# Reordering the opening of a cross-attention and expert kernel: the second key sums, the norms' product, the first tile's values

## The reference

```
q, k, v = ln(x) @ Wq.T + bq,  ctx @ Wk.T + bk,  ctx @ Wv.T + bv      (16 heads of 8)
scores = where(mask, float_min, q @ k.T / sqrt(8))                    (1024 x 6404)
x = x + (softmax(scores) @ v merged) @ Wo.T + bo
x = x + experts(ln(x))      (top 2 of 8, hidden width 512, gelu)
```

## Time and profile before

| | us |
|---|---|
| median of 3 runs | 332.46 (331.86 to 334.14) |
| the profiled execution | 330.95 |
| its span, first to last instruction | 329.3 |
| busy in the span: PE / DVE / ACT / POOL | 267.3 / 176.7 / 230.0 / 80.5 |

### The profile page before, as it was taken

One profiled execution on the slowest core, in us unless ns is written; L12 is line 12 of the kernel. 1 busy time (PEld: TensorE's weight loads), 2 busy tenths in 40 slices (PEclk: granted clock), 3 DMA queues, 4 the chain that ended last, 5 costly groups with the idle time before them and its releaser, 6 DMA issues.

```text
span 329.3 us, 6448 instructions
## 1 busy us (share of the span) xinstructions
PE 267.3 (81%) x1941; PEld 134.8 (41%) x1944; DVE 176.7 (54%) x431; ACT 230.0 (70%) x366; POOL 80.5 (24%) x137
## 2 busy tenths in 40 slices
PE   2689978989999989898989898966777577799940
PEld 2455534122121212121222222254666577798940
DVE  4799864354535363535454535476963125677612
ACT  4458856999999999999999999716951212555520
POOL 8891013000000000100010004030387105344430
PEclk9999999999999999999999999999979597999995
DMA  7999580101010101010100101895011521100115
GB/s 214 360 402 404 195 178 6 41 2 40 0 40 12 28 12 28 12 28 14 26 21 19 26 14 28 304 317 89 17 49 51 145 57 35 32 29 30 34 36 187
DMA packets 29011, 29.31 MB, mean 89 GB/s; under 512 B 15341, under 2 KB 22913, under 8 KB 28864
## 3 DMA queue, kind: packets, MB, share of 16 engines
q1 hardware_dynamic: 27536, 26.21, 26.2%
q0 software_dynamic: 1456, 2.86, 2.9%
HBM read 21.62 MB, written 7.45 MB: 88 GB/s over the span
## 4 chain that ended last, share of the span: by engine, by line
PE 45%; ACT 19%; issue 16%; DVE 11%; DMA 3%; another core or an unknown queue 2%; DVEq 2%; ACTq 1%; POOL 0%; POOLq 0%; SPq 0%
PE bank L1385 12%; ACT w2T L1073 10%; PE bank L1367 7%; PE bank L1494 6%; PE bank L1502 3%; PE bank L1235 3%; ACT arenaB L1073 3%; PE bank L1512 2%; PE bank L1196 2%; DVE arenaB L949 1%; PE bank L1261 1%; ACT w1T L1099 1%; ACT w2T L1099 1%; DMA x_sb<-in_x_dram 1%
## 5 line engine op out<-in xcount | busy, mean ns | idle before, releaser
L756 DVE TENSOR_TENSOR arenaA<-bank,arenaA 128x512 f32<-128x512 f32 x80 | 55.2, 691 | 80.0 <-PE bank L1385 80.0
L1073 ACT ACTIVATE arenaB<-bank 128x1024 f32<-128x1024 f32 x80 | 77.5, 1021 | 2.8 <-PE bank L1367 0.7
L1073 ACT ACTIVATE w2T<-bank 128x1024 f32<-128x1024 f32 x80 | 76.6, 1029 | 3.4 <-PE bank L1367 2.9
L1367 PE MATMUL bank<-qS,keys 64*128 64x512 bf16 x328 | 62.7, 386 | 10.7 <-ACT w2T L1073 7.6
L1106 ACT ACTIVATE mask_u<-bank,arenaB 128x128 f32<-128x128 f32 x92 | 26.3, 369 | 46.5 <-PE bank L1494 41.7
L1367 PEld LDWEIGHTS bank<-qS,keys 64*128 64x128 bf16 x328 | 15.5, 92 | 98.0 <-ACT w2T L1073 51.4
L1385 PE MATMUL bank<-arenaB,vcur 128*32 128x512 f32 x320 | 42.6, 604 | 2.8 <-DVE vcur L749 2.6
L1385 PE MATMUL bank<-w2T,vcur 128*32 128x512 f32 x320 | 42.6, 605 | 0.0
L411 POOL CAST keep<-flags 128x1 f32 x12 | 2.3, 189 | 161.1 <-DVE arenaC L649 139.6
L1494 PE MATMUL bank<-arenaB 128*128 128x128 f32 x184 | 28.1, 302 | 10.9 <-DVE arenaB L941 9.9
L1494 PEld LDWEIGHTS bank<-arenaB 128*128 128x128 f32 x184 | 24.7, 209 | 13.2 <-DVE arenaB L941 11.9
(11 more groups left out here) (318 smaller groups left out, 349.0 us busy)
## 6 DMA issues: line engine op xcount, KB each, us to landing
mask_u<-in_L_ffn_w_dram SPq DMA_DIRECT2D x2, 2048.0 KB, 10.5
mask_u<-in_mask_BxSxS_bk_dram SPq DMA_DIRECT2D x6, 560.5 KB, 12.6
ctx_sb<-in_ctx_dram SPq DMA_DIRECT2D x3, 768.0 KB, 13.4
qS<-qparts_dram SPq DMA_DIRECT2D x4, 448.0 KB
mask_u<-in_mask_BxSxS_bk_dram SPq DMA_DIRECT2D x6, 240.0 KB, 10.8
keys_in<-kparts_dram SPq DMA_DIRECT2D x40, 32.0 KB
mask_u<-in_mask_BxSxS_bk_dram SPq DMA_DIRECT2D x1, 1121.0 KB, 7.5
qparts_dram<-arenaA SPq DMA_DIRECT2D x2, 512.0 KB, 8.1
```

The costliest lines, as they stand in the source:

```text
L756: nc.vector.tensor_tensor(a, bank[:, 4 + k % 2, :], a, ALU.add).then_inc(s["ac"], 1)
L1073: nc.scalar.activation(probs[u % 8], bank[:, 2 * (u % 2):2 * (u % 2) + 2, :].rearrange("p a b -> p (a b)"), ACT.Exp, scale=SCALE).then_inc ...
L1367: last = mm(bank[:, 2 * (u % 2) + a, :], keys[rows, g, :], qS[rows, g, cols], start=not hides, stop=True, tile_position=(64 * a, 0))
```

## The change

The change reorders the stretch between the last chunks and the loop.

- The second key sums stand ahead of the last chunk's product (step 13 instead of 14) and lose the three fill-in matmuls around them.
- ScalarE no longer clears a part of `accU` at step 11: groups 1 to 3 are cleared in one instruction behind the last chunk.
- The norms' product stands ahead of the first tile's keys.
- The first tile's values are made behind L1284 in bank 3 (columns 128 to 255) instead of bank 6 behind the loads; VectorE's `value_parts` takes the place to read from as an argument, and its copy `vsrow` out of the same bank waits for `kv` too.
- The two loads stand ahead of the second half of `first_keys`.
- `hide(1)` stands behind `products(0)` and waits for the values (`vn`) and `cs_sb`.

```diff
--- before.py
+++ after.py
@@ -642,16 +642,16 @@
                 dve.wait_ge(read, i * 16 * KEY_DMAS + 16 * KEY_DMAS)
                 nc.vector.tensor_copy(keys[:, :, :].bitcast(F32), keys_in[:, :, :].bitcast(F32)).then_inc(copied, 1)
 
-            def value_parts(i):
+            def value_parts(i, products):
                 dve.wait_ge(s["kp"], 2 * i + 2)
                 dve.wait_ge(s["kv"], i + 1)
                 nc.vector.tensor_copy(vnext[:, :, HD:HD + 1], keep[:, :].rearrange("p (h a) -> p h a", h=1).broadcast_to([P, H, 1]))
-                nc.vector.scalar_tensor_tensor(vnext[:, :, 0:HD], b6[:, 2 * P:3 * P].rearrange("p (h d) -> p h d", d=HD), keep[:, :],
+                nc.vector.scalar_tensor_tensor(vnext[:, :, 0:HD], products.rearrange("p (h d) -> p h d", d=HD), keep[:, :],
                                                bvk[:, :].rearrange("p (h d) -> p h d", d=HD), ALU.mult, ALU.add).then_inc(s["vn"], 1)
 
             def parts(i):
                 key_parts(i, s["kv"], i + 1, s["kch"])
-                value_parts(i)
+                value_parts(i, b6[:, 2 * P:3 * P])
 
 
             dve.wait_ge(s["bd_ps"], 2)
@@ -678,12 +678,13 @@
             dve.wait_ge(s["rowkey"], len(COMBOS) + 4)
             nc.vector.tensor_tensor(shift_col[:, :], bank[:, 2, 64:65], shift_rows[:, :], ALU.mult).then_inc(s["bias"], 1)
             dve.wait_ge(s["cs_ps"], 1)
+            dve.wait_ge(s["kv"], 1)
             nc.vector.tensor_copy(vsrow[:, :], bank[0:1, 3, 0:P]).then_inc(s["cs_sb"], 1)
             dve.wait_ge(s["mt"], 2)
             nc.vector.tensor_copy(maskT[:, 0, :], maskT_ps).then_inc(s["mc"], 1)
             dve.wait_ge(s["cs_ps"], 2)
             nc.vector.tensor_copy(vsumB[:, :], bank[:, 3, 0:P]).then_inc(s["cs_sb"], 1)
-            value_parts(0)
+            value_parts(0, bank[:, 3, P:2 * P])
             dve.wait_ge(s["gen_ready"], 1)
             partial = dve.value_load(plan[0:1, 66:67], min_val=0, max_val=T)
             n = dve.value_load(plan[0:1, 64:65], min_val=1, max_val=T)
@@ -1025,9 +1026,6 @@
             for c in range(CHUNKS + 1):
                 if c == 1:
                     zero_sums(0, 1)
-                if c == 11:
-                    act.wait_ge(s["q_sb"], 4)
-                    zero_sums(1, 2)
                 if c == 2:
                     act.wait_ge(s["qk_ps"], 2)
                     nc.scalar.activation(ext[:, 0:2 * XE + QT * E], bank[:, 7, 0:2 * XE + QT * E], ACT.Copy).then_inc(s["qk_sb"], 1)
@@ -1049,9 +1047,10 @@
                     if c >= 3:
                         act.wait_ge(s["kn_ps"], c - 2)
                     nc.scalar.activation(squares[:, (c - 1) % 2, 0:w], bank[:, 6 + (c - 1) % 2, 0:w], ACT.Square, bias=qk_col[:, 1:2]).then_inc(s["sqr"], 1)
+            act.wait_ge(s["q_sb"], 4)
             act.wait_ge(s["qw"], 16 * len(Q_RUNS))
             act.wait_ge(s["qn_ps"], 1)
-            zero_sums(2, 4).then_inc(s["ac"], 1)
+            zero_sums(1, 4).then_inc(s["ac"], 1)
             act.wait_ge(s["plan_ready"], 1)
             first = act.value_load(plan[0:1, 0:1], min_val=0, max_val=T - 1)
             act.wait_ge(s["bd"], 7)
@@ -1217,13 +1216,12 @@
                     pe.wait_ge(s["qk_sb"], 2)
                 if c == 10:
                     key_sums(0)
-                if c == CHUNKS + 1:
+                if c == CHUNKS:
                     pe.wait_ge(s["kb_sb"], 1)
                     pe.wait_ge(s["bd"], 1)
                     pe.wait_ge(s["pick"], 1)
-                    keep_busy(bank[:, 2, :], 2)
                     key_sums(1)
-                    keep_busy(bank[:, 7, :], 1)
+                if c == CHUNKS + 1:
                     plan_counts()
                 if c < CHUNKS:
                     context_turn(c)
@@ -1275,13 +1273,15 @@
 
             pe.wait_ge(s["plan_ready"], 1)
             tile0 = pe.value_load(plan[0:1, 0:1], min_val=0, max_val=T - 1)
+            pe.wait_ge(s["bd"], 6)
+            mm(bank[0:1, 2, 0:H], norms[:, 2:3], ident[0:H, 0:H], start=True, stop=True).then_inc(s["bd_ps"], 1)
             pe.wait_ge(s["cc_sb"], CHUNKS)
             mm(b6[:, P:2 * P], wk_turned[:, :], ctx_sb[:, bass.ds(tile0, 1), :].rearrange("p a k -> p (a k)"), start=True, stop=True).then_inc(s["k_first"], 1)
-            pe.wait_ge(s["bd"], 6)
-            mm(bank[0:1, 2, 0:H], norms[:, 2:3], ident[0:H, 0:H], start=True, stop=True).then_inc(s["bd_ps"], 1)
             pe.wait_ge(s["cs_sb"], 1)
             pe.wait_ge(s["pl_sb"], 15)
             mm(bank[0:1, 3, 0:P], csT[:, :], wT[:, 2, :], start=True, stop=True).then_inc(s["cs_ps"], 1)
+            pe.wait_ge(s["cb"], 1)
+            mm(bank[:, 3, P:2 * P], cT[:, :], wT[:, 2, :], start=True, stop=True).then_inc(s["kv"], 1)
 
             def first_keys(g0, g1):
                 for gg in range(g0, g1):
@@ -1301,12 +1301,10 @@
             pe.wait_ge(s["s2"], 1)
             mm(bank[:, 3, 0:P], ones[0:1, 0:P], vsrow[0:1, :], start=True, stop=False)
             mm(bank[:, 3, 0:P], s2row[0:1, :], brow[0:1, 2, :], start=False, stop=True).then_inc(s["cs_ps"], 1)
-            first_keys(4, G)
             pe.wait_ge(s["gen_ready"], 1)
             partial = pe.value_load(plan[0:1, 66:67], min_val=0, max_val=T)
             general = pe.value_load(plan[0:1, 65:66], min_val=0, max_val=1)
-            pe.wait_ge(s["cb"], 1)
-            project_values().then_inc(s["kv"], 1)
+            first_keys(4, G)
             with pe.If(general):
                 n_max = pe.value_load(plan[0:1, 64:65], min_val=1, max_val=T)
                 pe.wait_ge(s["mc"], 1)
@@ -1388,12 +1386,13 @@
 
             pe.wait_ge(s["mc"], 1)
             hide(0, 0)
-            pe.wait_ge(s["cs_sb"], 3)
-            hide(1, 0)
             pe.wait_ge(s["qr"], 64)
             pe.wait_ge(s["qzero"], 2)
             pe.wait_ge(s["kc"], 1)
             products(0, True)
+            pe.wait_ge(s["cs_sb"], 3)
+            pe.wait_ge(s["vn"], 1)
+            hide(1, 0)
             products(1, True)
             pe.wait_ge(s["kc"], 2)
             pe.wait_ge(s["vn"], 1)
```

## The result

| | before | changed |
|---|---|---|
| median of runs, us | 332.16 (331.14 to 334.14, 4 runs) | 328.35 (328.05 to 328.86, 4 runs) |
| profiled execution, us (span) | 330.95 (329.3) | 328.86 (327.2) |
| busy share PE, DVE, ACT, POOL | see the section on the profile before | 82, 54, 70, 25% |

The ratio of the mean times is 0.988, with a 95% interval of 0.9831 to 0.9928. By the medians the change gains 3.8 us (2.4 to 5.6 by the interval); I had forecast 2.45, 330.0, and a range whose low end was 328.7. The direction was right, the size was not. Chips differ more than the kernels do: the unchanged kernel takes 320 us on two of them. Disturbed executions, some per cent slower, are left out of the ratios, and one chip has so many in every kernel (near 330, beside some near 320 to 324) that it gives none.

The account below looks back on a forecast made before the run. Bound taken: a chain of exponentials on ScalarE, so each microsecond won before the first one, at 54.20, comes off the end. 1.77 - 0.10 + 0.33 + 0.45 = 2.45 us, 332.46 to 330.0; range 328.7 to 332.0.

Parts of the forecast that it names:

- Plan 1.77 earlier: End of the chunk stage: memset moved and key sums earlier make the plan of tiles ready 1.77 us earlier, at 44.5.
- A matmul's wait holds the sequencer: Plan to first mask matmul: the values' product waits for POOL's copy and delays TensorE's sequencer steps behind it, cost 0.1 us.
- Rival 1: Plan to loop: a matmul's wait does not hold the sequencer, so loads and branch come sooner; gain 3.0, 329.5 us; chance 0.15.
- the forecast of 1.67 for L1295: Plan to first mask matmul: L1295 starts at 47.2 against 48.89, 1.67 us earlier, where the rest would have allowed 1.8.
- Loads ahead of the 24 instructions, +0.33: Before the branch: loads ahead of the first keys' second half save 0.84, less 0.1 and 0.4 for handing over: 0.33 us.
- the 2.0 forecast: Before the hides: semaphore step that lets ScalarE copy the keys at 50.25 to 50.4 against 52.3, first hide 2.0 us earlier.
- Second hide, +0.45: Loop's start: two hide matmuls instead of four stand before the first products, 0.45 us more gained.
- Rival 4: Opening, 42 to 45 us: without three fill-ins TensorE's clock falls to 1.2 GHz; slower by 4.5, 337 us; chance 0.04.
- Rivals 2 and 3: Loads lie bare 1.3 us before the keys' second half, 331.3, chance 0.12; a later wait takes the gain, 332.2, 0.12.
- the hand-over: TensorE's sequencer before the branch: 24 instructions handed over at 0.013 to 0.02 us each; 26 ns each takes 0.3 off.

Follow-up runs that it names:

- loads_late: Changed kernel with its two loads put back behind the second half of the first keys: 330.58 us, ratio 0.9966.
- after_fill: Changed kernel with six more fill-in matmuls between the second key sums and the tile's number: 328.55 us, ratio 0.9833; on a quieter chip 318.10, 0.9921.
- end_only: Kernel before with only the end of the chunk stage changed (memset, key sums, fill-ins): 321.43 us, ratio 1.0027; again on another chip 321.25, 0.9997.

## Why the prediction was wrong in size

- **Plan 1.77 earlier: right.** On one chip it is 1.69 (45.81 to 44.12). Over all profiles it stands at 45.81 to 46.47 in the unchanged kernel and at 44.12 and 44.42 in the changed one without a fall. Key sums at 40.43 and 40.52 (forecast 40.7) start 0.36 behind the end of VectorE's cast; in the third profile they come at 40.72, behind TensorE's own product.
- **A matmul's wait holds the sequencer: right, at 0.1 to 0.2 instead of 0.1.** The load of n ran at 46.2, together with the values' product at 46.25, which had waited for POOL's copy. Rival 1 falls as a mechanism. Its figure, a gain of 3.0 with the branch over before the keys' end, is what the opening shows, but by another way, so that is chance. With the rival falls the rule of the Trainium skill (Perfetto Trace Analysis, the per-instruction lifecycle of TensorE), as far as steps of the sequencer itself go. VectorE's step behind the bound (L672) came 1.90 earlier (48.69 to 46.79) and L1295 only 1.71 (48.62 to 46.91), so it is held by 0.2 in this profile (0.1 in the third). The chain from the plan to the bound had become as much shorter (2.88 to 2.67 from L617 to L672), and the forecast of 1.67 for L1295 held by this balance. The values' product ends at 46.74, well before the vsrow copy at 47.40, whose added wait costs nothing.
- **Loads ahead of the 24 instructions, +0.33: this is the step that failed.** I read the 0.84 ahead of the first load as the time to hand over 32 instructions, and so charged 0.3 to 0.5 for 24 of them behind the loads. It was a wait until the array began the first of them; behind the loads the 24 cost 0.1 at most. I had the evidence in the trace: the load at 50.6 ran when L1302's first matmul began, a row that I had not set beside it:
```profile
50.55 0.48 PE L1302 MATMUL bank<-arenaC,ones 1*128 1x128 f32 x2
```
  The run that reverts this step alone puts it at 0.69. With what is won between L1295 and the value sums it is 0.86 by the key copy, which came 2.56 earlier (52.17 to 49.61) against the 2.0 forecast. Branch at 49.1, not 49.8 to 49.95.
- **Second hide, +0.45: right**, 0.44.
- **Sum.** 1.71 + 0.86 + 0.43 = 3.0 at the exponential (53.96 to 50.96), against 2.45. The medians gave 3.8, 3.3 and 3.6 in three measurements, the ratios 4.0, 3.0 and 3.5, and 3.0 lies in each of their intervals; the difference is not settled.
- **Rival 4, the clock: the fall is real, at a smaller price, and what lets it come is not shown.** I had argued that the change makes the stretch denser. It does from the plan on, but it makes 40.8 to 44.2 emptier. In the changed kernel the fall comes in one of three profiles, lasts 3.4 us and costs 0.6 to 0.9 (exponential at 51.89 instead of 50.96 or 51.28), so the sign never turned. In the half that ends the chunk stage alone it lasts 6.9 us and costs 2.5, more than that half gains.
- **Rivals 2 and 3** are out: the loads do not lie bare (the second half of the keys starts at 49.07 instead of 51.19), and nothing in the loop takes the gain back, though loads_late is 2.0 above after_fill in the median for a step of 0.7, a difference that I cannot part into step and clock.
- **The range.** I bounded the hand-over from one side only (26 ns each, which takes 0.3 off) and gave no bound to its being almost free. That alone does not put the result outside: 332.46 - 3.0 is 329.5, inside the range of 328.7 to 332.0. The measured 328.35 lies another 1.1 lower: 0.8 because the medians show 3.8 and not 3.0, and 0.3 because the median before came out at 332.16. No run puts the 0.8 down to a step; by the interval (2.4 to 5.6) it can be chance.

## What to carry to other kernels

Before a wait of a sequencer is priced as so many instructions handed over, ask which matmul began at that moment: if one did, the wait may be one for room, and the load belongs ahead of what fills it. Two parts of a change can be worth more together than apart, here a loss of 0.9 and a gain of 2.0 against a gain of 3.0: with the end alone the clock fell for some 7 us in both profiles, with both parts for 3.4 in one of three, and why is not shown. Judge such parts together. And read the time of one opening in several executions of the same program before a difference of a microsecond is put down to an edit.

## What the runs showed of the hardware that I had not expected

- A register load of TensorE's sequencer stood until the first of the 32 array instructions directly ahead of it began: 49.1 and 49.05 in loads_late, 50.3 and 50.29 in the unchanged kernel, 49.7 and 49.72 in end_only. Handing over 24 instructions took about 0.1 us when there was room.
- The granted clock of one program in one stretch differs between executions: the changed kernel has 0.50 from 43.4 to 46.8 in one profile and 1.00 in two others, and the kernel with only the end changed stood at the lower level for 6.9 us in one and 6.8 us in the other. Of the profiles with the three fill-ins ahead of the plan one in eight falls before the loop, of those without them five in nine.
- The same kernel takes 328.35 us in one measurement and 316.6 to 316.75 on two other chips, a difference three times the change. Ratios on one chip agree (0.988, 0.9907, 0.9891).
